# A decoder layer's flags for empty low halves: from TensorE and ScalarE to one GpSimd reduction

## What is computed

```python
q = (x @ (codes_q * scales_q)) + bq          # k, v alike; 16 heads of 128; scales shared by 32 rows
scores = einsum('bqhd,bkhd->bhqk', q, k) / sqrt(128)
x = layernorm(x + (softmax(scores) @ v) @ (codes_o * scales_o) + bo)
x = layernorm(x + cross_attention(x, ctx))   # 1024 context rows, top 54 scores kept
x = layernorm(x + (silu(x @ wg.T) * (x @ wu.T)) @ wd.T)
```

## Time and profile before

| | |
|---|---|
| time, median of 3 runs | 960.34 us (960.02 to 960.86) |
| the profiled execution | 959.64 us, its span 957.8 us |
| TensorE busy | 924.8 us, 97% |
| VectorE, ScalarE busy | 576.4 us, 581.8 us |
| GpSimd busy | 477.4 us, 377 instructions |
| the product with ones, L762 | 60 matmuls from 38.1 to 487.2 us |
| ScalarE's total, L1080 | 30 activations, 30 accumulator reads |

### The profile page before, as it was taken

One profiled execution on the slowest core, in us unless ns is written; L12 is line 12 of the kernel. 1 busy time (PEld: TensorE's weight loads), 2 busy tenths in 40 slices (PEclk: granted clock), 3 DMA queues, 4 the chain that ended last, 5 costly groups with the idle time before them and its releaser, 6 DMA issues.

```text
span 957.8 us, 13371 instructions
## 1 busy us (share of the span) xinstructions
PE 924.8 (97%) x4516; PEld 752.0 (79%) x4516; DVE 576.4 (60%) x1055; ACT 581.8 (61%) x1203; POOL 477.4 (50%) x377
## 2 busy tenths in 40 slices
PE   8999999999999999999999999899999899999997
PEld 7787778878788787877677787888878788888885
DVE  4666856576666666565675799984878214521114
ACT  4657876687767778687875446544565634443333
POOL 3256652536615456466664357553674651364440
PEclk9999999999999999999999999989999999999999
DMA  6532230122200312222222122332433341243331
GB/s 199 154 92 64 73 99 1 41 77 72 84 17 28 89 59 69 64 64 69 54 67 88 53 58 88 89 100 55 132 113 96 91 130 44 91 129 94 94 87 45
DMA packets 46103, 76.99 MB, mean 80 GB/s; under 512 B 5584, under 2 KB 11216, under 8 KB 45776
## 3 DMA queue, kind: packets, MB, share of 16 engines
q1 hardware_dynamic: 45600, 75.68, 27.2%
q10 hardware_dynamic: 432, 0.39, 0.2%
HBM read 73.69 MB, written 2.36 MB: 79 GB/s over the span
## 4 chain that ended last, share of the span: by engine, by line
PE 80%; DVE 9%; ACT 6%; issue 4%; DMA 1%; POOL 0%; SPq 0%; ACTq 0%; DVEq 0%; POOLq 0%
PE p L934 6%; PE p L938 6%; PE p L935 6%; PE p L691 5%; PE p L726 5%; PE p L693 4%; PE p L736 3%; PE p L740 3%; PE p L737 3%; PE p L713 3%; PE p L948 3%; PE p L950 3%; PE p L949 3%; PE p L673 2%; PE p L669 2%
## 5 line engine op out<-in xcount | busy, mean ns | idle before, releaser
L1546 DVE TENSOR_SCALAR_CACHE_REDUCE JK<-p,ssc 128x512 bf16<-128x512 f32 x112 | 83.9, 749 | 142.4 <-PE p L673 142.4
L2108 POOL TENSOR_TENSOR acc<-SX,acc 128x512 f32<-128x512 f32 x54 | 71.4, 1322 | 172.5 <-ACT SX L1101 130.5
L2025 POOL TENSOR_TENSOR V<-RAW,V 128x512 fp32r<-128x512 f32 x64 | 82.9, 1317 | 140.8 <-ACT V L1121 140.8
L1063 ACT ACTIVATE PR<-p,nms,ssc 128x512 f32<-128x512 f32 x112 | 87.4, 780 | 56.7 <-DVE JK L1546 56.1
L691 PE MATMUL p<-R 128*128 128x512 f32 x248 | 97.4, 393 | 1.0 <-DVE V L1539 0.8
L2025 POOL TENSOR_TENSOR C<-RAW,C 128x512 fp32r<-128x512 f32 x58 | 76.2, 1326 | 40.0 <-ACT C L1121 39.8
L1860 DVE TENSOR_TENSOR SX<-p,SX 128x512 f32<-128x512 f32 x32 | 22.1, 692 | 114.3 <-PE p L938 108.4
L1559 DVE TENSOR_TENSOR PT<-p,PT 128x512 fp32r<-128x512 f32 x128 | 87.5, 683 | 4.7 <-ACT PT L1086 4.6
L726 PE MATMUL p<-ident,PR 128*128 128x128 f32 x512 | 78.3, 275 | 0.4
L1086 ACT ACTIVATE PT<-p 128x512 fp32r<-128x512 f32 x128 | 75.7, 592 | 0.7 <-PE p L726 0.7
L693 PE MATMUL p<-R 128*128 128x512 f32 x192 | 75.1, 391 | 0.0
(11 more groups left out here) (252 smaller groups left out, 2688.6 us busy)
## 6 DMA issues: line engine op xcount, KB each, us to landing
RAW<-in_wg SPq DMA_DIRECT2D x32, 256.0 KB, 2.9
RAW<-in_wu SPq DMA_DIRECT2D x32, 256.0 KB, 2.7
RAW<-in_ctxn SPq DMA_DIRECT2D x32, 256.0 KB, 2.9
RAW<-in_wd SPq DMA_DIRECT2D x32, 256.0 KB, 2.8
RAW<-in_wq SPq DMA_DIRECT2D x19, 256.0 KB, 2.7
RAW<-in_wk SPq DMA_DIRECT2D x18, 256.0 KB, 2.7
RAW<-in_wv SPq DMA_DIRECT2D x16, 256.0 KB, 2.9
RAW<-in_wo SPq DMA_DIRECT2D x16, 256.0 KB, 4.8
```

The lines of the kernel that those rows point to most:

```text
L1063: e.activation(PR[:, i % 2, :], P[i % 2][:, :], ACT.Exp, bias=nms[:, i % 4:i % 4 + 1], scale=ssc[:, 0:1] if HB[j][0] > 1 else SC, accum_ou ...
L1546: e.tensor_scalar(JK[:, :], P[i % 2][:, :], ssc[:, 1:2] if HB[i // 4][0] > 1 else -SC, None, ALU.mult, ALU.min, accum_out=nms[:, i % 4:i % ...
L2025: e.tensor_tensor(lo, RAW[:, slot[key], :], hi, ALU.subtract).then_inc(*c_lo.up(key))
```

## The change

The flag is made by one GpSimd instruction, a reduction by maximum over all axes, partitions included, of `mag`'s columns of a key into `flag`. TensorE's product with ones, its PSUM bank, ScalarE's total and the semaphore between the two are gone. The early and late tables become one, `TOTALS`: all keys are reduced in the first iteration behind the one of their last look, and on GpSimd the reduction stands behind the multiplications of its iteration. For the o keys that had an early sum that is one iteration sooner than before. ScalarE's look waits, for the first piece of a key, until the flag that last used the same column group of `mag` has been made.

```diff
+            for item in list(full):
+                if item[0] < i:
+                    full.remove(item)
+                    totals.setdefault(i, []).append(item[1])
...
-        for key in SUMS_EARLY.get(i, []) + SUMS_LATE.get(i, []):
-            take("sum", key)
...
-            def add_lows(key):
-                n, c = low_size(key), LOWCOL[key] % 4
-                w.wait_ge(*low_abs.at(LOWPIECES[key][-1]))
-                ps = claim(BANK["sum", key], low_flag, key)
-                e.matmul(ps[0:1, 0:n], ones[:, 0:1], mag[:, c, 0:n], start=True, stop=True).then_inc(*low_sum.up(key))
...
+                if n == 0 and c >= 4:
+                    w.wait_ge(*low_flag.at(KEYAT[c - 4]))
                 e.activation(JA[:, :], halves_of(piece)[1], ACT.Abs,
                              accum_out=mag[:, c % 4, n:n + 1]).then_inc(*low_abs.up(piece))
-
-            def low_total(key):
-                c, n = LOWCOL[key], low_size(key)
-                w.wait_ge(*low_sum.at(key))
-                e.activation(fsum[:, 0:n], P[BANK["sum", key]][0:1, 0:n], ACT.Copy,
-                             accum_out=flag[:, c:c + 1]).then_inc(*low_flag.up(key))
...
+            def low_total(key):
+                c, n = LOWCOL[key], low_size(key)
+                w.wait_ge(*low_abs.at(LOWPIECES[key][-1]))
+                e.tensor_reduce(flag[0:1, c:c + 1], mag[:, c % 4, 0:n], ALLAXES, ALU.max).then_inc(*low_flag.up(key))
...
                 for piece in pieces_at(i):
                     multiply(piece)
+                for key in TOTALS.get(i, []):
+                    low_total(key)
                 if j in (1, 3):
                     add_bias(2 * (j - 1) + qt, "bo1")
```

More of the change, by code:

```diff
@@ L12 @@
 AX = mybir.AxisListType.X
+ALLAXES = mybir.AxisListType.XYZWC
 NB, S, D = 2, 512, 512
@@ L192, in low_plan @@
     queue = [(-1, ("v", 0, kt)) for kt in range(4)]
-    looks, early, late, col, seen, full = {}, {}, {}, {}, {}, []
+    looks, totals, col, seen, full = {}, {}, {}, {}, []
     for i in range(-1, 4 * NJ):
         if i >= 0:
[L196 to L203, removed]
+            for item in list(full):
+                if item[0] < i:
+                    full.remove(item)
+                    totals.setdefault(i, []).append(item[1])
         for _ in range(2):
@@ L214, in low_plan @@
             queue += [(i, piece) for piece in pieces_at(i - 2)]
-    return looks, early, late, col, seen
-LOOKS, SUMS_EARLY, SUMS_LATE, LOWCOL, LOWPIECES = low_plan()
+    return looks, totals, col, seen
+LOOKS, TOTALS, LOWCOL, LOWPIECES = low_plan()
+KEYAT = {c: key for key, c in LOWCOL.items()}
 def ring_plan():
@@ L314, in decoder_layer @@
         mag = sbt(top, "mag", [128, 4, 4])
-        fsum = sbt(top, "fsum", [1, 4])
         flag = sbt(top, "flag", [1, 32])
@@ L424, in decoder_layer @@
         x_hi, x_lo = sig("x_hi"), sig("x_lo")
-        low_abs, low_sum, low_flag = sig("low_abs"), sig("low_sum"), sig("low_flag")
+        low_abs, low_flag = sig("low_abs"), sig("low_flag")
         proj, qk_hi, qk_lo = sig("proj"), sig("qk_hi"), sig("qk_lo")
@@ L822, in tensor @@
                     proj_v(*v_tile(i))
-                for key in SUMS_EARLY.get(i, []):
-                    add_lows(key)
                 if qt < 3:
@@ L828, in tensor @@
                     scores(i + 2)
-                for key in SUMS_LATE.get(i, []):
-                    add_lows(key)
                 if bias_at(i) is not None:
@@ L1265, in scalar @@
                     v_high(*v_tile(i))
-                for key in SUMS_EARLY.get(i, []):
-                    low_total(key)
                 if qt < 3:
                     pt_high(i)
-                for key in SUMS_LATE.get(i, []):
-                    low_total(key)
                 if i + 2 < 4 * NJ:
```

## The result

The changed kernel takes 968.96 us (median of 4 runs, 965.86 to 970.78), the kernel before 960.18 (4 runs): a ratio of 1.0097, 95% interval 1.0080 to 1.0114, so 8.8 us slower. I had forecast 976.5 in a range of 962 to 1015. The profiled execution took 965.86 us, 6.2 more than that of before.

A forecast was written before the change was run, and what follows sets the result against it. TensorE was taken as the bound: 13.6 us of sums saved, but about 30 us of stalls on flags late in GpSimd's queue, net +16.8 on 959.64, so 976.5 us, range 962 to 1015.

The follow-up runs named there:

- e2_mid: The changed kernel with GpSimd's reduction put behind the addition and ahead of the low halves and multiplications; 955.7 us, ratio 0.9958.
- e6_fill: The changed kernel with 37 useless TensorE matmuls ahead of the flag loads of the five keys with the longest stalls; 963.94 us, ratio 1.0045.
- e7_ring: The changed kernel with PSUM banks handed out as in the kernel before, the sums' banks taken but unused; 974.09 us, ratio 1.0159.

## What to carry to other kernels

A small operation moved to an engine with half its time free costs what stands ahead of it in that engine's queue, less the slack, and little by its own duration; work out, key by key, when the queue gets to it and when the result is needed, and put it where its input ends, which here was worth some 20 us for two moved lines. Price a stall of the bounding engine with the clock behind it as well. And when a step leaves a shared ring, check whether the slot that it gives up is part of the gain.

## What was not expected of the hardware

- GpSimd's reduction over 128 partitions takes 0.32 us for two columns and for four (299 to 332 ns, 30 of them; a single one in e2_mid took 772 ns), and several in a row start down to 0.18 us apart.
- From the end of a write on GpSimd to the matmul behind a register load on TensorE it is 0.50 to 0.52 us in the changed kernel, and 0.39 to 0.40 for the five keys of e6_fill ahead of which TensorE had been kept busy. Why is open.
- The same stalls of TensorE (3.1 and 2.7 us) were followed by a lower clock in one execution (0.59 over the 3.4 us from 447.00) and not in another of the same kernel. In e7_ring one of 1.89 us was, too.
